# Attention and spectral feed-forward on one core: two weighted sums of a block issued back to back, and three GpSimd steps in other places

## The chip, the cores and the metric

One core of a Trainium2 chip runs the whole program. The time is the device time of one execution in microseconds (us). Engine names in the rows: PE is TensorE, PEld its weight loads, DVE is VectorE, ACT is ScalarE, POOL is GpSimd, SP is SyncE.

## The reference, cut to what matters

Two batches of 2048 tokens of width 512 attend to 128 context tokens with 16 heads, and a linear layer in the frequency domain follows; both have a layer norm ahead and a residual.

```python
q = layernorm(x) @ wq + bq;  k = ctx @ wk + bk;  v = ctx @ wv + bv       # 16 heads of 32
score = where(q k^T / sqrt(32) * mask == 0, -1e9, q k^T / sqrt(32) * mask)
x = x + (softmax(score) @ v) @ wo + bo
y = real(ifft(fft(layernorm(x)) @ (w_real + i w_imag)))                  # one real 512 x 512 matrix
x = x + y + bias
```

## The kernel before

The tokens are cut into 16 blocks (c = 0 to 15) of 256. A block has 4 **groups** of 4 heads, numbered s = 4c + g over the whole program, 64 in all. All large products are split into float16 high and low parts (names ending in h and l), three products for one.

The order of work is written out by hand. `plan()` makes a table of **slots** v, one for each group and some before and behind; four slots, r = v mod 4 = 0 to 3, make one block's period. Each engine's program loops over the same slots and has its own list of steps in each. A group s passes through them so:

- PE computes its scores (`scores`, L628) in slot s - 1 into the tile `scores`, of which there is one. DVE multiplies by the mask (`mask_mul`, L970), replaces zeros (`zero_to_neg`, L977, both inputs in SBUF) and takes minima (`least`, L982) in slot s. GpSimd turns the minima into `nbias` (`bias`, L1264). ACT takes exponentials (`exps`, L745, two calls of four instructions) in slot s + 1; one half of them lies before, the other behind the copies named next.
- PE transposes the result (`turn`, L642) in slot s + 2, and ACT copies it to `pt` (`copy_pt`, L754).
- Two groups make one **context** m = s // 2: PE forms the weighted sum of values (`weigh`, L656; eight fp32 products with 32 columns each, which the trace shows as 16 records) in slot 2m + 3, so one in each slot with r = 1 and r = 3. It goes to a PSUM bank of its own, `CX`. The reciprocals of the row sums are taken by DVE (L988), spread by GpSimd (`spread`, L1271, tile `rzb`), transposed by PE (the fill "R", L584) and copied by ACT (`copy_rec`, L761). In slot 2m + 5 DVE multiplies (`ctx_norm`, L995, tile `cn`), ACT casts to the high half (`ctx_hi`, L768, tile `ch`), GpSimd forms the low half (`ctx_lo`, L1277, tile `cl`).

Between these PE runs **fills**, each a group of products into one of three PSUM banks taken in turn, so that fill n may start only when the bank of fill n - 3 has been read by DVE (semaphore `g_free`, counted in the order of fills). In one period they are: r = 0: "WO" 0 and "R"; r = 1: "WO" 1 and "QQ"; r = 2: "FF" 0 and "R"; r = 3: "FF" 1, for most blocks "ST", and "QQ". "WO" is the output projection of block c - 2 (L478, 12 products), "FF" the feed-forward of block c - 3 (L478), "QQ" the query projection of a later block (L483, 24 products), "ST" a small product of statistics (L491). A fill "QQ" is read in the slot behind its own: ACT casts it to `qh` (L719), and then DVE forms `ql` (L942), which frees the bank.

GpSimd's other steps are the sums with the bias of the output projection (`add_bo`, L1216, on `xs`), with the last bias (`add_bf`, L1250, on `x1`), low halves (`split_lo` L1207, `norm_lo2` L1239), and small ones for the statistics (`rstd2`: L1223 and L1226). In slots 4 to 63 it waits for `zero_to_neg` of the slot before most of its steps.

Of the kernel before, what the change touches and what calls it, by code (L numbers as in the profile page):

```python
# [5 lines left out]
ALU = mybir.AluOpType  # L6
# [31 lines left out]
def plan():  # L38

    fills, slots, held = [], {}, []
    lead = [("CT", 0), ("CT", 1), ("K", 0), ("K", 1), ("W1", 0), ("ST", 0), ("Q", 0, 0), ("Q", 0, 1), ("S", 0),
            ("W1", 1), ("Q", 0, 2), ("Q", 0, 3), ("S", 1), ("ST", 1), ("Q", 1, 0), ("Q", 1, 1), ("S", 2),
            ("Q", 1, 2), ("Q", 1, 3)]
    front = []
    for f in lead:
        if f[0] == "S":  # L50
# [8 lines left out]
    }  # L59
    queries = {2: (2, 0), 4: (2, 1), 5: (3, 0), 6: (3, 1)}  # L60
    for v in range(V0, V1):
        c, r = divmod(v, 4)
        mid = {
            0: [("WO", c - 2, 0)],
            1: [("WO", c - 2, 1)],
            2: [("FF", c - 3, 0)],
            3: [("FF", c - 3, 1)],
        }[r]
        mid = [f for f in mid if 0 <= f[1] < NC] + early.get(v, [])
        mid = {NS - 4: [("FF", NC - 4, 0)], NS - 3: [("WO", NC - 3, 1)], NS - 2: [], NS - 1: [("FF", NC - 3, 0)],  # L70
               NS: [("WO", NC - 2, 0)], NS + 1: [("WO", NC - 2, 1)], NS + 2: [("FF", NC - 3, 1)], NS + 3: []}.get(v, mid)
# [12 lines left out]
        if v in queries:  # L84
            late.append(("QQ",) + queries[v])
        elif v >= 7 and v % 2 == 1 and (v + 9) // 4 < NC:
            late.append(("QQ", (v + 9) // 4, (v + 9) % 4 // 2))
        base = len(fills)
        fills += mid + late
        mids = list(range(base, base + len(mid)))  # L90
        lates = list(range(base + len(mid), len(fills)))
        items = []
        if 0 <= v - 2 < NS:
            items += [("PT", v - 2, 0), ("PT", v - 2, 1)]
        items += [("G", n) for n in mids]
        if 0 <= v + 1 < NS:
            items += [("S", v + 1, 0), ("S", v + 1, 1)]
        if v % 2 == 1 and 0 <= v - 3 < NS:
            items += [("PV", (v - 3) // 2)]
        items += [("G", n) for n in lates]  # L100
        slots[v] = (items, [n for n in held if fills[n][0] in ("R", "ST")],
                    [n for n in held if fills[n][0] not in ("R", "ST")], [n for n in mids if fills[n][0] != "R"])
        held = lates
    return fills, front, slots


def row_slot(c):
# [21 lines left out]
def build(nc, x, xt, ctx_in, mask, wq, bq, wk, bk, wv, bv, wo, bo, lparts, tables, bf, eye, sums, pick, places, heads, out):  # L129
# [3 lines left out]
    with ExitStack() as stack:  # L133
# [337 lines left out]
        def _(pe):  # L471
# [22 lines left out]
            def fill(n):  # L494
# [84 lines left out]
                elif kind == "R":  # L579
                    pe.wait_ge(p_rz, c + 1)  # L580
                    for i in range(2):
                        for t in range(2):
                            a = 256 * i + 128 * t
                            last = pe.transpose(o[:, a:a + 128], rzb[:, i, 4 * t:4 * t + 4, :], ident[:])  # L584
                elif kind == "WO":
                    pe.wait_ge(o_lo, 2)
                    pe.wait_ge(ch_done, min(2 * c + 2, NS // 2 - 1))
# [54 lines left out]
                        last = pe.transpose(PB[f][:, a:a + 128], zs[:, s % NZ, t, 2 * f + i, :], ident[:])  # L642
                last.then_inc(pt_done, 1)

            def weigh(m):
                c, h = divmod(m, 2)
                b = c // (NC // NB)
                pe.wait_ge(pt_copied, 4 * m + 4)
                if m >= 1:
                    pe.wait_ge(cn_done, m)  # L650
                else:
                    pe.wait_ge(g_free, at["V", 0] + 1)
                for i in range(2):
                    for j in range(4):
                        n = 32 * (8 * h + 4 * i + j)
                        last = pe.matmul(CX[32 * j:32 * j + 32, 256 * i:256 * i + 256], vs[:, b, n:n + 32],  # L656
                                         pt[:, i, j, :], start=True, stop=True)
                last.then_inc(pv_done, 1)

            def zeros(count):  # L660
                for i in range(count):
# [17 lines left out]
        def _(act):  # L679
# [69 lines left out]

            def copy_pt(s, f):  # L750
                act.wait_ge(pt_done, 2 * s + f + 1)
                if f == 0 and s >= 2:
                    act.wait_ge(pv_done, s // 2)
                act.copy(pt[:, s % 2, 2 * f:2 * f + 2, :], PB[f][:]).then_inc(pt_copied, 1)  # L754

            def copy_rec(m):
                n = at["R", m]
                act.wait_ge(g_done, n + 1)
                if m >= 1:
                    act.wait_ge(cn_done, m)  # L760
                act.copy(rec[:], bank_of(n)[:].rearrange("p (i n) -> p i n", i=2)).then_inc(rc_done, 1)  # L761

            def ctx_hi(m):
                c, h = divmod(m, 2)
                act.wait_ge(cn_done, m + 1)
# [58 lines left out]
            for v in range(V0, V1):  # L824
# [35 lines left out]
                    exps(v - 1, 1)  # L860
                if v == 8:
                    exps(v, 0)
                if v % 2 == 1 and 0 <= v - 5 < NS - 2:
                    ctx_hi((v - 5) // 2)
                if v == NS + 1:
                    norm_hi2(NC - 2, 0)
                    copy_rec(NS // 2 - 1)
                    norm_hi2(NC - 2, 1)
                    last_ctx_hi()
# [16 lines left out]
        def _(dve):  # L886
# [102 lines left out]

            def ctx_norm(m):  # L990
                dve.wait_ge(rc_done, m + 1)
                dve.wait_ge(pv_done, m + 1)
                if m >= 1:
                    dve.wait_ge(p_cl, m)
                dve.tensor_tensor(cn[:], CX[:].rearrange("p (i n) -> p i n", i=2), rec[:], ALU.mult).then_inc(cn_done, 1)  # L995

            def last_ctx_norm():
                m = NS // 2 - 1
                dve.wait_ge(rc_done, m + 1)
                dve.wait_ge(pv_done, m + 1)  # L1000
# [105 lines left out]
            for v in range(V0, V1):  # L1106
# [3 lines left out]
                    mask_mul(v)  # L1110
                if v == NS + 1:
                    recip(NS // 2 - 1)
                if v % 2 == 1 and 0 <= v - 5 < NS - 2:
                    ctx_norm((v - 5) // 2)
                for n in prompt:
                    lo(n)
                if 0 <= v < NS:
# [57 lines left out]
        def _(pool):  # L1175
# [166 lines left out]
            for v in range(V0, V1):  # L1342
# [37 lines left out]
                for a in range(5, NC):  # L1380
                    if v == 4 * a - 11 and v != 13:
                        split_lo(a, slice(0, 2), False)
                    if v == 4 * a - 10 and v != 14:
                        split_lo(a, slice(2, 4))
                for a in range(2, 14):
                    if bo_slot(a) == v:
                        add_bo(a, 0)
                if v == 52:
                    add_bo(12, 1)
# [184 lines left out]
```

## Time and profile before

| | |
|---|---|
| time, median of 3 runs (lowest to highest) | 437.15 us (437.01 to 437.19) |
| the profiled execution: time, span | 437.58 us, 435.8 us |
| busy: PE, DVE, ACT, POOL | 430.0, 398.6, 365.2, 355.4 us |
| granted TensorE clock | 1.00 of full speed |

Busy is the time in which at least one instruction of the engine ran. The span is the time from the first to the last instruction of the profiled execution. A start in a timeline is counted from the start of the span; an instruction's time on DVE, ACT and POOL overlaps the start of the next one by up to 0.1 us, so steps are best read from start to start.

### The profile page before, as it was taken

What the parts mean: (1) busy time and instruction counts of PE and PEld (TensorE: products, weight loads), DVE (VectorE), ACT (ScalarE), POOL (GpSimd) and SP (SyncE); (2) the same over time, 40 slices, a digit from 0 to 9 for tenths busy, and PEclk for the clock granted to TensorE, in tenths of its full rate; (3) what the DMA queues carried; (4) which work ended last, traced back from release to release, by engine and by line L of the source; (5) the groups of instructions that cost most, each with busy time, mean ns of one, the idle gap of its engine ahead of it and who ended that gap; (6) DMA issues with size and microseconds to landing.
All of it is one profiled execution on the core that took longest, in us unless ns stands there. A gap on an engine that the chain in (4) does not pass through costs nothing.

```text
span 435.8 us, 10928 instructions
## 1 busy us (share of the span) xinstructions
PE 430.0 (99%) x3496; PEld 298.5 (69%) x3496; DVE 398.6 (91%) x535; ACT 365.2 (84%) x1341; POOL 355.4 (82%) x484
## 2 busy tenths in 40 slices
PE   7999999999999999999999999999999999999997
PEld 6897688787766776667676677666667765656544
DVE  3799899999999999999999999999999899999663
ACT  1768998989898999999899998999898898999820
POOL 5579988877999898989989898989899865675793
DMA  8999854403443855455455454445442434231144
GB/s 272 396 386 250 299 168 121 117 0 98 101 136 91 200 96 145 123 126 138 125 146 138 126 144 121 100 118 148 109 110 68 102 85 106 72 98 49 50 114 128
DMA packets 85286, 60.15 MB, mean 138 GB/s; under 512 B 40141, under 2 KB 72813, under 8 KB 84718
## 3 DMA queue, kind: packets, MB, share of 16 engines
q1 hardware_dynamic: 84508, 59.29, 49.6%
q8 instruction: 29, 0.48, 0.5%
q14 instruction: 27, 0.22, 0.2%
q10 hardware_dynamic: 722, 0.17, 0.2%
HBM read 29.33 MB, written 8.39 MB: 87 GB/s over the span
## 4 chain that ended last, share of the span: by engine, by line
PE 94%; DVE 2%; ACT 1%; issue 1%; POOL 1%; DVEq 0%; POOLq 0%
PE bank L478 36%; PE bank L483 24%; PE bank L642 12%; PE bank L656 7%; PE scores L628 6%; PE bank L584 3%; PE bank L565 2%; PE scores L483 1%; PE bank L662 1%; ACT zs L745 1%; PE bank L491 1%; DVE zs L977 1%; DVE nmin L982 0%; PE bank L505 0%; ACT pt L754 0%
## 5 line engine op out<-in xcount | busy, mean ns | idle before, releaser
L745 ACT ACTIVATE zs<-zs,nbias 128x128 f32<-128x128 f32 x512 | 199.7, 397 | 13.3 <-POOL nbias L1264 12.9
L745 ACT ACTIVATION_READ_ACCUMULATOR zs<-zs,nbias 128x1 f32 x512 | 99.4, 194 | 0.0
L977 DVE SCALAR_TENSOR_TENSOR zs<-zs 128x1024 f32<-128x1024 f32 x64 | 88.9, 1389 | 1.1
L982 DVE TENSOR_REDUCE nmin<-zs 128x8 f32<-128x1024 f32 x64 | 78.0, 1219 | 2.1
L970 DVE TENSOR_TENSOR zs<-scores,ms 128x1024 f32<-128x1024 f32 x64 | 78.0, 1218 | 0.1
L754 ACT COPY pt<-bank 128x512 f32<-128x512 f32 x128 | 67.9, 582 | 8.2 <-PE bank L642 8.0
L642 PE MATMUL bank<-ident,zs 128*128 128x128 f32 x512 | 66.7, 273 | 0.1
L1216 POOL TENSOR_TENSOR xs<-xs,bob 128x512 f32<-128x512 f32 (+1 forms) x41 | 43.4, 1059 | 22.9 <-DVE zs L977 22.8
L483 PE MATMUL bank<-xth,wqh 128*128 128x256 f16 x224 | 61.2, 273 | 0.0
L483 PE MATMUL bank<-xth,wql 128*128 128x256 f16 x224 | 61.1, 273 | 0.0
L483 PE MATMUL bank<-xtl,wqh 128*128 128x256 f16 x224 | 61.1, 273 | 0.0
L642 PEld LDWEIGHTS bank<-ident,zs 128*128 128x128 f32 x512 | 57.6, 140 | 3.6 <-ACT zs L745 1.7
L478 PE MATMUL bank<-woh,ch 128*128 128x512 f16 x128 | 48.5, 379 | 0.6 <-POOL cl L1277 0.6
L478 PE MATMUL bank<-wol,ch 128*128 128x512 f16 x128 | 48.5, 379 | 0.0
L478 PE MATMUL bank<-woh,cl 128*128 128x512 f16 x128 | 48.5, 379 | 0.0
L478 PE MATMUL bank<-mh,x1h 128*128 128x512 f16 x120 | 45.5, 379 | 0.0
L478 PE MATMUL bank<-ml,x1h 128*128 128x512 f16 x120 | 45.5, 379 | 0.0
L478 PE MATMUL bank<-mh,x1l 128*128 128x512 f16 x120 | 45.5, 379 | 0.0
L1239 POOL TENSOR_TENSOR x1nl<-x,x1nh 128x512 f16<-128x512 f32 x30 | 35.8, 1194 | 9.6 <-DVE zs L977 9.6
L1250 POOL TENSOR_TENSOR x<-x,bfb 128x512 f32<-128x512 f32 x32 | 41.1, 1286 | 1.4 <-DVE zs L977 1.2
L628 PEld LDWEIGHTS scores<-ks,qs 102*128 102x128 f16 (+1 forms) x480 | 31.9, 98 | 13.2 <-issue 0.2
L1271 POOL COPY rzb<-rz 128x512 f32<-128x512 f32 x32 | 38.5, 1202 | 2.0 <-DVE rz L988 1.7
(130 smaller groups left out, 906.3 us busy)
## 6 DMA issues: line engine op xcount, KB each, us to landing
xs<-in_x SPq DMA_DIRECT2D x16, 512.0 KB, 4.4
xtr<-in_xt SPq DMA_DIRECT2D x16, 512.0 KB, 4.8
out<-x SPq DMA_DIRECT2D x31, 256.0 KB, 2.5
qs<-qh SPq DMA_DIRECT2D x120, 64.0 KB
lp<-in_lparts SPq DMA_DIRECT2D x4, 1024.0 KB, 9.8
qs<-ql SPq DMA_DIRECT2D x60, 64.0 KB
ms<-in_mask SPq DMA_DIRECT2D x16, 128.0 KB, 2.4
wks<-in_wk SPq DMA_DIRECT2D x2, 512.0 KB, 6.2
```

Of the source, the lines that this page charges most:

```text
L478: last = pe.matmul(o, a, b, start=(i == 0), stop=(i == len(mm) - 1))
L483: last = pe.matmul(o, a, b, start=(first and i == 0), stop=(i == len(pairs) - 1))
L628: last = pe.matmul(A[:, n % 2, 128 * j:128 * j + 128], qs[c % 2][0:rows, g, j, 128 * t:128 * t + 128], ks[0:rows, g, j, c // (NC // NB), : ...
L642: last = pe.transpose(PB[f][:, a:a + 128], zs[:, s % NZ, t, 2 * f + i, :], ident[:])
L745: last = act.activation(z, z, ACT.Exp, bias=nbias[:, s % 4, i:i + 1], scale=-NEG, accum_out=zsum[:, s % 4, i:i + 1])
L754: act.copy(pt[:, s % 2, 2 * f:2 * f + 2, :], PB[f][:]).then_inc(pt_copied, 1)
L970: dve.tensor_tensor(zs[:, s % NZ], A[:].rearrange("p t (h k) -> p t h k", h=4), ms[:, c % NM].unsqueeze(2).broadcast_to([128, 2, 4, KEYS]) ...
L977: dve.scalar_tensor_tensor(out=z, in0=z, scalar=0.0, in1=z, op0=ALU.is_equal, op1=ALU.subtract).then_inc(eq_done, 1)
L982: dve.tensor_reduce(nmin[:, s % 4, :], zs[:, s % NZ].rearrange("p t h k -> p (t h) k"), AX.X, ALU.min).then_inc(mn_done, 1)
L1216: i = pool.tensor_tensor(z, z, bob[:, n], ALU.add)
L1250: pool.tensor_tensor(z, z, bfb[:], ALU.add).then_inc(p_x1b, 1)
L1271: pool.tensor_copy(rzb[:].rearrange("p i h w -> p (i h) w"), rz[:, z, :].rearrange("p i h -> p (i h)").unsqueeze(2).broadcast_to([128, 16, ...
```

## The change

For blocks 3 to 12 the weighted sum of the first context (m = 2c) no longer stands in slot 4c + 3. It is now a fill "P" in slot 4c + 5, straight ahead of the weighted sum of the second context (m = 2c + 1), and writes to one of the three banks that the fills share; the second still goes to `CX`. A second buffer `ptb` holds the transposed exponentials of every other context. `ctx_norm`, `ctx_hi` and `ctx_lo` of the first context move one slot on, from 4c + 5 to 4c + 6. On GpSimd `ctx_lo` of the second context now stands ahead of `bias` in slot 4c + 7; `add_bo(c, 0)` of blocks 4 to 11 moves from slot 4c + 3 to slot 4c + 5, and `add_bf(c - 3, 1)` from r = 1 to r = 2.

```diff
+PAIRED = range(3, 13)
+LATE_BO = range(4, 12)
...
+        both = [("P", (v - 5) // 4)] if r == 1 and (v - 5) // 4 in PAIRED else []
...
-        fills += mid + late
+        fills += mid + both + late
...
+        items += [("G", base + len(mid))] * len(both)
-        if v % 2 == 1 and 0 <= v - 3 < NS:
+        if v % 2 == 1 and 0 <= v - 3 < NS and not in_fill((v - 3) // 2):
             items += [("PV", (v - 3) // 2)]
...
+def in_fill(m):
+    return m % 2 == 0 and m // 2 in PAIRED
...
+def in_pair_end(v):
+    return v % 4 == 3 and (v - 7) // 4 in PAIRED
...
+def late_bf(v):
+    return VT <= v < NS or v // 4 - 1 in LATE_BO
...
+        ptb, _ = sb("ptb", [128, 2, 4, CH], F32, a_wv)
+        pts = [pt, ptb]
...
+                elif kind == "P":
+                    last = weighted(2 * c, o)
...
-                if f == 0 and s >= 2:
-                    act.wait_ge(pv_done, s // 2)
+                if f == 0 and s >= 4:
+                    wait_weighed(act, s // 2 - 2)
...
-                if v % 2 == 1 and 0 <= v - 5 < NS - 2:
+                if v % 2 == 1 and 0 <= v - 5 < NS - 2 and not in_fill((v - 5) // 2):
                     ctx_hi((v - 5) // 2)
+                if v % 2 == 0 and in_fill((v - 6) // 2):
+                    ctx_hi((v - 6) // 2)
...
+                if v % 2 == 0 and in_fill((v - 6) // 2):
+                    ctx_norm((v - 6) // 2)
...
+                if in_pair_end(v):
+                    ctx_lo((v - 5) // 2)
                 for a in range(2, 14):
-                    if bo_slot(a) == v:
+                    if bo_slot(a) == v and a not in LATE_BO:
                         add_bo(a, 0)
...
+                if v % 2 == 0 and in_fill((v - 6) // 2):
+                    ctx_lo((v - 6) // 2)
...
+                if r == 1 and c - 1 in LATE_BO:
+                    add_bo(c - 1, 0)
-                if r == 2 and VT <= v < NS:
+                if r == 2 and late_bf(v):
                     add_bf(c - 3, 1)
```

The order of instructions on three engines shows where this puts them. The line numbers of the changed kernel are other ones: 668 for 628, 692 for 656, 521 for 483, 788 for 745, 797 for 754, 811 for 768, 762 for 719, 780 for 737, 804 for 761, 1325 for 1277, 1312 for 1264, 1287 for 1239, 1264 for 1216, 1319 for 1271.

On PE, in slot 33 (r = 1), from the last scores on; before:

```order
L478 MATMUL bank<-woh,cl 128x512
L628 MATMUL scores<-ks,qs_63 128x128 x8
L656 MATMUL bank<-pt,vs 32x256 x8
L483 MATMUL bank<-xth,wqh 128x256
L483 MATMUL bank<-xth,wql 128x256
```

and of the change:

```order
L516 MATMUL bank<-woh,cl 128x512
L668 MATMUL scores<-ks,qs_63 128x128 x8
L692 MATMUL bank<-pt,vs 32x256 x8
L692 MATMUL bank<-ptb,vs 32x256 x8
L521 MATMUL bank<-xth,wqh 128x256
```

Eight products more stand between the scores and "QQ"; in slot 35 (r = 3) the same eight are gone from between the scores and "ST".

On ACT, in slot 34 (r = 2), from the copies of `pt` on; before:

```order
L754 COPY pt<-bank 128x512 x2
L745 ACTIVATE zs,zsum<-zs,nbias 128x128 x4
L719 CAST qh<-bank 128x512
L737 CAST x1nh<-x_76 128x512
L761 COPY rec<-bank 128x512
```

and of the change:

```order
L797 COPY pt<-bank 128x512 x2
L788 ACTIVATE zs,zsum<-zs,nbias 128x128 x4
L811 CAST ch<-cn 128x512
L762 CAST qh<-bank 128x512
L780 CAST x1nh<-x_76 128x512
L804 COPY rec<-bank 128x512
```

The cast of `ch` (`ctx_hi` of the first context) now stands ahead of the cast of `qh`; it is gone from slot 33.

On POOL, the end of slot 34 and slot 35 (r = 3); before:

```order
L1239 TENSOR_TENSOR x1nl<-x_76,x1nh 128x512
L1216 TENSOR_TENSOR xs<-xs,bob 128x256
L1216 TENSOR_TENSOR xs<-xs,bob 128x512
L1264 TENSOR_SCALAR nbias<-nmin 128x8
L1277 TENSOR_TENSOR cl<-cn,ch 128x512
L1239 TENSOR_TENSOR x1nl<-x_76,x1nh 128x512
L1216 TENSOR_TENSOR xs<-xs,bob 128x256
L1271 COPY rzb<-rz 128x512
```

and of the change:

```order
L1325 TENSOR_TENSOR cl<-cn,ch 128x512
L1287 TENSOR_TENSOR x1nl<-x_76,x1nh 128x512
L1298 TENSOR_TENSOR x_76<-x_76,bfb 128x512
L1264 TENSOR_TENSOR xs<-xs,bob 128x256
L1325 TENSOR_TENSOR cl<-cn,ch 128x512
L1312 TENSOR_SCALAR nbias<-nmin 128x8
L1287 TENSOR_TENSOR x1nl<-x_76,x1nh 128x512
L1264 TENSOR_TENSOR xs<-xs,bob 128x256
L1319 COPY rzb<-rz 128x512
```

Slot 34 has a low half `cl` and an `add_bf` more. In slot 35 the sum of 512 columns on `xs` is gone, and the second context's `cl` stands ahead of `nbias`.

## Rows read from the trace of the kernel before

**Rows 1.** The page's engines, and its chain that ended last, by engine.

```profile
PE 430.0 (99%) x3496; PEld 298.5 (69%) x3496; DVE 398.6 (91%) x535; ACT 365.2 (84%) x1341; POOL 355.4 (82%) x484
...
PE 94%; DVE 2%; ACT 1%; issue 1%; POOL 1%; DVEq 0%; POOLq 0%
```

**Rows 2.** Windows of one period: length, busy per engine, clock, DMA.

```profile
243.07:267.17 24.10, 24.10 (x205) 16.50 (x203) 23.43 (x31) 22.00 (x83) 21.32 (x29) 1.00 0.48 129
```

**Rows 3.** Timeline, PE, slots 32 to 37: start, us, line, operation.

```profile
226.33 0.61 PE L628 MATMUL scores<-ks,qs 102*128 102x128 f16 x8
226.78 0.60 PE L584 MATMUL bank<-ident,rzb 128*128 128x128 f32 x4
...
230.68 0.61 PE L628 MATMUL scores<-ks,qs 102*128 102x128 f16 x8
231.22 1.07 PE L656 MATMUL bank<-pt,vs 128*32 128x256 f32 x16
232.23 0.28 PE L483 MATMUL bank<-xth,wqh 128*128 128x256 f16 x1
...
234.86 1.04 PE L642 MATMUL bank<-ident,zs 128*128 128x128 f32 x8
...
252.19 0.38 PE L478 MATMUL bank<-woh,ch 128*128 128x512 f16 x1
...
254.78 0.39 PE L628 MATMUL scores<-ks,qs 102*128 102x128 f16 x4
```

**Rows 4.** Timeline, PE, first half of the sum at 231.22.

```profile
231.22 0.64 PE L656 MATMUL bank<-pt,vs 128*32 128x256 f32 x8
```

**Rows 5.** Timeline, ACT, slots 34 to 36; idle before in brackets.

```profile
238.00 0.57 ACT L719 CAST qh<-bank 128x512 f16<-128x512 f32 x1
...
239.41 0.59 ACT L761 COPY rec<-bank 128x512 f32<-128x512 f32 x1 [0.32 <-PE bank L584]
...
244.06 0.61 ACT L768 CAST ch<-cn 128x512 f16<-128x512 f32 x1
...
245.28 0.40 ACT L745 ACTIVATE zs<-zs,nbias 128x128 f32<-128x128 f32 x1 [0.33 <-POOL nbias L1264]
...
247.60 1.07 ACT L754 COPY pt<-bank 128x512 f32<-128x512 f32 x2 [0.68 <-PE bank L642]
...
250.11 0.57 ACT L719 CAST qh<-bank 128x512 f16<-128x512 f32 x1
```

**Rows 6.** Timeline, POOL, slot 35.

```profile
245.01 0.23 POOL L1264 TENSOR_SCALAR nbias<-nmin 128x8 f32<-128x8 f32 x1
245.21 1.16 POOL L1277 TENSOR_TENSOR cl<-cn,ch 128x512 f16<-128x512 f32 x1
246.32 1.16 POOL L1239 TENSOR_TENSOR x1nl<-x,x1nh 128x512 f16<-128x512 f32 x1
247.45 0.72 POOL L1216 TENSOR_TENSOR xs<-xs,bob 128x256 f32<-128x256 f32 x1
```

**Rows 7.** Timeline, DVE, slots 34 to 37.

```profile
238.61 0.69 DVE L942 TENSOR_TENSOR ql<-bank,qh 128x512 f16<-128x512 f32 x1
...
240.70 1.22 DVE L970 TENSOR_TENSOR zs<-scores,ms 128x1024 f32<-128x1024 f32 x1
...
246.33 1.23 DVE L970 TENSOR_TENSOR zs<-scores,ms 128x1024 f32<-128x1024 f32 x1
247.59 1.66 DVE L977 SCALAR_TENSOR_TENSOR zs<-zs 128x1024 f32<-128x1024 f32 x1
...
250.72 0.69 DVE L942 TENSOR_TENSOR ql<-bank,qh 128x512 f16<-128x512 f32 x1 [0.21 <-ACT qh L719]
...
252.88 1.23 DVE L970 TENSOR_TENSOR zs<-scores,ms 128x1024 f32<-128x1024 f32 x1
```

**Rows 8.** One line's instructions (L977, L1271): count, ns min/median/max.

```profile
L977 DVE SCALAR_TENSOR_TENSOR zs<-zs x64: 1215/1228/2311, 25.8 to 401.6; 128x1024 f32<-128x1024 f32 x64
...
L1271 POOL COPY rzb<-rz x32: 602/1602/1617, 48.9 to 411.9; 128x512 f32<-128x512 f32 x32
```

More of the change, by code:

```diff
@@ L87, in plan @@
             late.append(("QQ", (v + 9) // 4, (v + 9) % 4 // 2))
+        both = [("P", (v - 5) // 4)] if r == 1 and (v - 5) // 4 in PAIRED else []
         base = len(fills)
-        fills += mid + late
+        fills += mid + both + late
         mids = list(range(base, base + len(mid)))
-        lates = list(range(base + len(mid), len(fills)))
+        lates = list(range(base + len(mid + both), len(fills)))
         items = []
@@ L104, in plan, with own @@
     return fills, front, slots
+def in_fill(m):
+    return m % 2 == 0 and m // 2 in PAIRED
+def own(m):
+    return m + 1 - sum(in_fill(i) for i in range(m + 1))
 def row_slot(c):
@@ L294, in cast_count, with wait_weighed, wait_context @@
             return n + 1 - min(n + 1, 2) - min(max(n + 1 - tile_of(12, 0), 0), 4)
+        def wait_weighed(eng, m):
+            if in_fill(m):
+                eng.wait_ge(g_done, at["P", m // 2] + 1)
+            else:
+                eng.wait_ge(pv_done, own(m))
+        def wait_context(eng, m):
+            if in_fill(m):
+                eng.wait_ge(g_free, at["P", m // 2] + 1)
+            else:
+                eng.wait_ge(cn_done, own(m))
         def columns(n):
@@ L643, in turn, with weighted @@
                 last.then_inc(pt_done, 1)
-            def weigh(m):
+            def weighted(m, o):
                 c, h = divmod(m, 2)
@@ L648, in weigh @@
                 pe.wait_ge(pt_copied, 4 * m + 4)
[L649 to L652, printed above, removed]
                 for i in range(2):
@@ L655, in weigh @@
                         n = 32 * (8 * h + 4 * i + j)
-                        last = pe.matmul(CX[32 * j:32 * j + 32, 256 * i:256 * i + 256], vs[:, b, n:n + 32],
-                                         pt[:, i, j, :], start=True, stop=True)
-                last.then_inc(pv_done, 1)
+                        last = pe.matmul(o[32 * j:32 * j + 32, 256 * i:256 * i + 256], vs[:, b, n:n + 32],
+                                         pts[m % 2][:, i, j, :], start=True, stop=True)
+                return last
+            def weigh(m):
+                if m >= 1:
+                    pe.wait_ge(cn_done, own(m) - 1)
+                else:
+                    pe.wait_ge(g_free, at["V", 0] + 1)
+                weighted(m, CX).then_inc(pv_done, 1)
             def zeros(count):
@@ L751, in copy_pt @@
                 act.wait_ge(pt_done, 2 * s + f + 1)
-                if f == 0 and s >= 2:
-                    act.wait_ge(pv_done, s // 2)
-                act.copy(pt[:, s % 2, 2 * f:2 * f + 2, :], PB[f][:]).then_inc(pt_copied, 1)
+                if f == 0 and s >= 4:
+                    wait_weighed(act, s // 2 - 2)
+                act.copy(pts[s // 2 % 2][:, s % 2, 2 * f:2 * f + 2, :], PB[f][:]).then_inc(pt_copied, 1)
             def copy_rec(m):
@@ L759, in copy_rec @@
                 if m >= 1:
-                    act.wait_ge(cn_done, m)
+                    wait_context(act, m - 1)
                 act.copy(rec[:], bank_of(n)[:].rearrange("p (i n) -> p i n", i=2)).then_inc(rc_done, 1)
@@ L764, in ctx_hi @@
                 c, h = divmod(m, 2)
-                act.wait_ge(cn_done, m + 1)
+                wait_context(act, m)
                 if h == 0 and c >= 2:
@@ L991, in ctx_norm @@
                 dve.wait_ge(rc_done, m + 1)
-                dve.wait_ge(pv_done, m + 1)
+                wait_weighed(dve, m)
                 if m >= 1:
                     dve.wait_ge(p_cl, m)
-                dve.tensor_tensor(cn[:], CX[:].rearrange("p (i n) -> p i n", i=2), rec[:], ALU.mult).then_inc(cn_done, 1)
+                src, done = (bank_of(at["P", m // 2]), g_free) if in_fill(m) else (CX, cn_done)
+                dve.tensor_tensor(cn[:], src[:].rearrange("p (i n) -> p i n", i=2), rec[:], ALU.mult).then_inc(done, 1)
             def last_ctx_norm():
@@ L999, in last_ctx_norm @@
                 dve.wait_ge(rc_done, m + 1)
-                dve.wait_ge(pv_done, m + 1)
+                dve.wait_ge(pv_done, own(m))
                 dve.wait_ge(p_cl, m)
@@ L1112, in _ @@
                     recip(NS // 2 - 1)
-                if v % 2 == 1 and 0 <= v - 5 < NS - 2:
+                if v % 2 == 1 and 0 <= v - 5 < NS - 2 and not in_fill((v - 5) // 2):
                     ctx_norm((v - 5) // 2)
+                if v % 2 == 0 and in_fill((v - 6) // 2):
+                    ctx_norm((v - 6) // 2)
                 for n in prompt:
@@ L1428, in _ @@
                     norm_lo2(c - 2, 0)
-                elif v % 2 == 1 and 2 <= v - 5 < NS - 2:
+                elif v % 2 == 1 and 2 <= v - 5 < NS - 2 and not in_fill((v - 5) // 2) and not in_pair_end(v):
                     ctx_lo((v - 5) // 2)
+                if v % 2 == 0 and in_fill((v - 6) // 2):
+                    ctx_lo((v - 6) // 2)
                 if v == NS + 1:
@@ L1441, in _ @@
                     norm_lo2(c - 2, 1)
-                if v not in (NS - 4, NS + 1) and r < 2 and 0 <= c - 3 < NC and v > 13 and not (r == 1 and VT <= v < NS):
+                if v not in (NS - 4, NS + 1) and r < 2 and 0 <= c - 3 < NC and v > 13 and not (r == 1 and late_bf(v)):
                     add_bf(c - 3, r)
-                if r == 2 and VT <= v < NS:
+                if r == 1 and c - 1 in LATE_BO:
+                    add_bo(c - 1, 0)
+                if r == 2 and late_bf(v):
                     add_bf(c - 3, 1)
```

## The prediction

> **What bounds the kernel now.** I read the page's engines and its chain first: PE is busy for 430.0 of 435.8 us and holds 94% of the chain [rows 1]. Then the windows of one period, four slots: 24.10 us, PE busy in all of it at full clock, but DVE busy for 23.43 and ACT for 22.00 [rows 2]. So a microsecond taken from PE is worth one only as far as DVE and ACT can come forward with it. The reader should look for that in the timelines: how much idle time they have, and how early they hand over what PE needs next. The place is "WO" 1 of r = 1 (slot 37). It needs the bank in which "QQ" of slot 35 lay, which DVE frees with `ql`. That ends at 250.72 + 0.69 = 251.41, and PE starts at 252.19: 0.78 us to spare [rows 3, 7]. The scores behind it (254.78) need the mask product that starts at 252.88 and ends at 254.11: 0.67 us [rows 3, 7]. I take this period for all ten.
>
> **What the change takes from PE.** In slot 35, "QQ" or "ST" follows the scores at once. Without a weighted sum, the next operation starts 0.45 us after the scores do (226.33 to 226.78), with one 1.55 (230.68 to 232.23) [rows 3]: 1.10 us gone. In slot 33, eight products more stand in a sum that is already under way. The first 8 of its 16 records end after 0.64 us and all 16 after 1.07 [rows 4, 3], so 8 records cost 0.43, 16 more 0.86; entering and leaving the narrow products is paid once. A period then has 1.10 - 0.86 = 0.24 us less on PE, and ten pairs 2.4 us. That is all the change can give.
>
> **What it does to the two others.** I count from the transpositions of r = 2, PE at 234.86, as zero, because ACT waits for them there before and after: with the pair ahead of "QQ" they come 0.86 later than other work of the slot.
>
> ACT: `qh` starts at 3.14 [rows 5]. The change puts `ch` (0.61, of which 0.10 overlaps the next) ahead of it: 3.65. DVE's `ql` follows `qh` by 0.61 (238.00 to 238.61), so it moves from 3.75 to 4.26 [rows 5, 7]. On ACT the delay is taken up soon: the copy of `rec` at 239.41 had 0.32 idle before it [rows 5], and about 0.1 of delay remains, which the wait for `nbias` behind it covers. The cast `ch` of the second context then stands where it stood, at 9.20. Behind it comes the moved step of GpSimd. Before, `nbias` started at 245.01 (10.15) and did not depend on `ch`; now the low half `cl` goes first and waits for `ch`. It ends at 9.81; I add 0.08 for the signal (an estimate: the ACT to DVE signal of the `ql` row is 0.04), 1.11 for `cl` (245.21 to 246.32), and have `nbias` at 11.00; exponentials follow 0.27 later (245.01 to 245.28) at 11.27, against 10.42 now [rows 5, 6]. That is 0.85 late. Four exponentials take 1.55 (from 245.28 to the idle time ahead of 247.60, less overlap), so the copy of `pt` starts at 12.8; now it starts at 12.74 after waiting 0.68 for PE [rows 5]. That wait is gone, as PE comes 1.10 earlier there, and `nbias` has eaten it. `qh` 2.51 later (247.60 to 250.11) and `ql` another 0.61 later stands at **15.95, against 15.86 now**.
>
> DVE has the same answer by its own row: `ql` at 4.26, 7.72 to the mask product of slot 36 (238.61 to 246.33), 1.26 to L977, then L977, L982 and `ql` [rows 7]. L977 is stretched there now, 1.66 where its least is 1.22 [rows 7, 8]. At its start (247.59) a GpSimd sum still ran until 248.17 [rows 6], 0.58 us, and the stretch is 0.44. After the change GpSimd's `rzb` copy of 0.60 [rows 8] should start about 0.25 ahead of L977 (`nbias` 11.00, then 0.2, 1.13 and 0.7 for the three steps behind it, 13.0; L977 at 13.24), so 0.37 is left of it and, with the same 0.14 off, the stretch is 0.23. Then `ql` cannot start before 15.86 either.
>
> The Trainium skill's page "SBUF — State Buffer", section "Who interferes with whom", says that a DVE instruction with two SBUF inputs and a GpSimd instruction that reads SBUF exclude each other for the whole instruction. By that rule the stretch would be all of the 0.37, DVE would be ready at 16.0, and the total would be 0.5 us higher. The row of L977 agrees that the two exclude each other, but shows 0.44 of stretch for 0.58 of overlap, so the sum keeps the 0.23.
>
> So neither row moves, while PE has lost 1.10 us ahead of "WO" 1. The scores of slot 38 would start at 254.78 - 234.86 - 1.10 = 18.82. Their mask product starts 2.16 after `ql` (250.72 to 252.88) [rows 7] and takes 1.23: 15.95 + 2.16 + 1.23 = 19.34, with 0.04 for a signal 19.38. PE waits some **0.55 us in each period**, most of it already ahead of "WO" 1 (16.68 against 16.23). Queued behind are the scores, the pair, "QQ" and the next transpositions, for which ACT waits: the loop closes, and each period starts from the same state. A period takes 24.10 - 0.24 + 0.55 = 24.41 us.
>
> **The sum.** Ten places: nine full periods between the first and the last pair at 0.55, and the first (slot 17), where `ch` and `cl` are not moved yet, at 0.35 (between nothing and 0.55). -2.4 + 9 x 0.55 + 0.35 = +2.9 us. The profiled execution took 437.58 us with a span of 435.8; the median of the runs is 437.15, to which I add: **440.0 us**. The signals (0.03 to 0.1) and the roundings of a long row make the wait 0.40 to 0.67, which gives 438.7 to 441.1 for this case.
>
> What I cost at nothing: the bank of "P", which "WO" 0 held a slot earlier and "R" needs again only a slot later; DVE's moved `cn`, as DVE then waits for `qh` anyway; the moved `add_bo` and `add_bf`, hidden by GpSimd's idle time (355.4 of 435.8 us busy [rows 1]), with `xs` and `x` read slots later (if GpSimd is late, see rival 4); the second buffer `ptb`, which only takes a wait away. No DMA is moved, and SP's queue has the same order.
>
> **Rivals.** (1) *Faster.* ACT and DVE come forward after all: 0.55 us less between the transpositions and `ql`, and PE waits nowhere: 434.8 us. For it: ACT has 1.33 us idle in this stretch (0.32, 0.33, 0.68) [rows 5]. Against it: each of the three is spent above on `ch` and `cl`, and DVE has only 0.21 idle [rows 7]. It decides where the wait is under 0.24 per period, what PE saves. (2) *No change:* the wait is 0.15 to 0.33, about half of what I work out: -2.4 and ten times that give 436.3 to 438.0. (3) *The pair does not share its way in and out*, since it writes two banks and reads two buffers: the first sum costs 1.10 instead of 0.86, and 24.41 becomes 24.65: 442.4 us. For it: no two such sums stand together in the trace. Against: the bank and the buffer do not matter to the products of L478, which change both without a gap. (4) *GpSimd runs into L977 in r = 3.* Slot 34 has a `cl` (1.16 [rows 6]) and an `add_bf` more on GpSimd, and by the same kind of steps its last sum on `xs` ends some 0.1 ahead of L977 of slot 35 (an estimate). If it is 0.2 late it is still free; each tenth beyond that costs a tenth, up to 0.6 (the 0.72 of that sum less 0.14), each period: up to 445 us.
>
> **Chances.** The forecast 0.53; (3) or (4), slower still, 0.12; (2) 0.14, of which some ends on either side; (1) 0.21. What a measurement can tell from no change is about 0.2%, 0.9 us. Slower by more 0.65, within it 0.14, faster by more 0.21. The range leaves out a tenth on each side: the lower end stands inside rival (1), with part of the waits left (435.4), the upper end at rival (3), 442.6.
>
> **What the profile after would show.** PE idle of about 0.4 ahead of L516's first product in r = 1 and 0.1 to 0.2 ahead of the scores, every 24.4 us; the removed sum leaving 0.45 between scores and "ST"; the pair taking 1.93 us from its first start to its last end; ACT without idle time from the copy of `pt` in r = 2 to `ch`, then about 1.2 us of waiting for `nbias`; `qh` 15.3 after the transpositions. I am wrong if PE stays without idle time and the period is 23.86, or if `nbias` in r = 3 is not behind `cl`.

## The result, and the profile after

| | before | after |
|---|---|---|
| time, median of 6 runs each (lowest to highest) | 437.08 us (436.55 to 437.22) | 444.21 us (443.08 to 445.48) |
| ratio, 95% interval | | 1.0167 [1.0142, 1.0191] |
| the profiled execution: time, span | 437.58, 435.8 us | 445.31, 443.5 us |
| granted TensorE clock of the profiled execution | 1.00 | 0.996 |

The change makes the kernel 7 us slower. I had forecast slower, but 440.0 us and 442.6 at most. The six runs of after fall in two groups: three have a granted clock of 0.996 (445.05, 445.31, 445.48 us) and three one of 1.0 (443.08, 443.18, 443.36 us). One of the sixteen runs of the kernel before that were taken beside e8 and e9 (below) took 905.53 us, and the ratios leave it out.

Read first the page's engines and its chain by engine, against [rows 1]:

```profile
PE 433.2 (98%) x3496; PEld 298.9 (67%) x3496; DVE 393.4 (89%) x535; ACT 362.4 (82%) x1341; POOL 348.2 (79%) x484
...
PE 49%; DVE 25%; ACT 10%; issue 10%; POOL 4%; DMA 1%; DVEq 0%; SPq 0%; ACTq 0%; POOLq 0%
```

PE held 94% of the chain and now holds 49%. DVE, ACT and POOL are no busier than before; they are later. The table of waits says for what (engine and line, what it waited for: us in total, times, longest):

```profile
ACT zs L788 <- POOL nbias L1312: 26.6, 24, 3.5
POOL cl L1325 <- ACT ch L811: 23.4, 21, 3.1
DVE ql L987 <- ACT qh L762: 17.0, 12, 3.5
```

Two of the three are the steps of the forecast: the exponentials behind `nbias`, and `cl` behind `ch`. The longest wait of the exponentials, 3.5 us, is far above the 1.2 that I worked out for one period. So I read a steady period and the last place apart. Windows of after: the period that answers to [rows 2], from the scores of slot 37 to those of slot 41, then the one from slot 53 to slot 57:

```profile
251.34:275.80 24.46, 24.35 (x203) 16.44 (x202) 22.94 (x31) 21.67 (x83) 20.24 (x30) 1.00 0.50 128
349.19:376.32 27.13, 24.38 (x193) 15.55 (x192) 20.96 (x27) 22.02 (x86) 15.40 (x23) 0.94 0.37 79
```

Eight such periods in a row, from the scores of slot 21 to those of slot 53, are 24.45 to 24.47 us long (forecast: 24.41). The last is 27.13, and its granted clock is 0.94.

The steady period on PE, from the scores of slot 37 on (timeline; compare [rows 3]):

```profile
251.34 0.61 PE L668 MATMUL scores<-ks,qs 102*128 102x128 f16 x8
251.79 0.61 PE L622 MATMUL bank<-ident,rzb 128*128 128x128 f32 x4
252.40 1.09 PE L682 MATMUL bank<-ident,zs 128*128 128x128 f32 x8
253.60 0.39 PE L516 MATMUL bank<-woh,ch 128*128 128x512 f16 x1
...
256.29 0.62 PE L668 MATMUL scores<-ks,qs 102*128 102x128 f16 x8
256.84 1.07 PE L692 MATMUL bank<-pt,vs 128*32 128x256 f32 x16
257.73 1.05 PE L692 MATMUL bank<-ptb,vs 128*32 128x256 f32 x16
```

The second sum starts 0.89 behind the first (0.86 forecast): the way in and out is shared. From "R" to the transpositions it is 0.61 us, on to "WO" 1 1.20, on to the scores 2.69. In a kernel without the wait (e6, below) these are 0.44, 0.88 and 2.59. PE therefore waits 0.17 + 0.32 + 0.10 = 0.59 us, little of which counts as idle time of PE: in the waits of this stretch it stands with the weight loads (0.2 for ACT's exponentials, 0.3 for `ql`, 0.4 for the mask product). The forecast had nothing ahead of the transpositions and about 0.45 ahead of "WO" 1.

ACT and POOL of the same stretch (compare [rows 5, 6]):

```profile
240.02 0.61 ACT L811 CAST ch<-cn 128x512 f16<-128x512 f32 x1
240.53 0.58 ACT L762 CAST qh<-bank 128x512 f16<-128x512 f32 x1
...
246.05 0.62 ACT L811 CAST ch<-cn 128x512 f16<-128x512 f32 x1
...
248.20 0.40 ACT L788 ACTIVATE zs<-zs,nbias 128x128 f32<-128x128 f32 x1 [1.26 <-POOL nbias L1312]
...
249.76 1.04 ACT L797 COPY ptb<-bank 128x512 f32<-128x512 f32 x2
...
252.25 0.57 ACT L762 CAST qh<-bank 128x512 f16<-128x512 f32 x1
```

```profile
246.81 1.16 POOL L1325 TENSOR_TENSOR cl<-cn,ch 128x512 f16<-128x512 f32 x1 [1.89 <-ACT ch L811]
247.94 0.23 POOL L1312 TENSOR_SCALAR nbias<-nmin 128x8 f32<-128x8 f32 x1
```

The transpositions of slot 34 start at 236.88 here. Counted from there `qh` comes at 15.37 (forecast 15.34). DVE (compare [rows 7]) has `ql` at 252.85, which is 15.97 (15.95), and L1022 takes 1.49 (1.45):

```profile
250.12 1.49 DVE L1022 SCALAR_TENSOR_TENSOR zs<-zs 128x1024 f32<-128x1024 f32 x1
...
252.85 0.69 DVE L987 TENSOR_TENSOR ql<-bank,qh 128x512 f16<-128x512 f32 x1
```

Now the last place, slots 51 to 54; POOL, ACT, and PE:

```profile
344.66 1.16 POOL L1325 TENSOR_TENSOR cl<-cn,ch 128x512 f16<-128x512 f32 x1 [0.85 <-ACT ch L811]
345.78 1.27 POOL L1264 TENSOR_TENSOR xs<-xs,bob 128x512 f32<-128x512 f32 x1
347.02 1.21 POOL L1312 TENSOR_SCALAR nbias<-nmin 128x8 f32<-128x8 f32 x1
```

```profile
348.25 0.40 ACT L788 ACTIVATE zs<-zs,nbias 128x128 f32<-128x128 f32 x1 [3.47 <-POOL nbias L1312]
```

```profile
350.05 0.63 PE L622 MATMUL bank<-ident,rzb 128*128 128x128 f32 x4 [0.24 <-POOL rzb L1319]
352.45 1.97 PE L682 MATMUL bank<-ident,zs 128*128 128x128 f32 x8 [1.78 <-ACT zs L788]
354.21 0.64 PE L516 MATMUL bank<-woh,ch 128*128 128x512 f16 x1
354.64 0.64 PE L516 MATMUL bank<-wol,ch 128*128 128x512 f16 x1
...
357.52 0.61 PE L668 MATMUL scores<-ks,qs 102*128 102x128 f16 x8
```

Between `cl` and `nbias` stands a sum of 512 columns that is in no other such slot: `add_bo(12, 0)`. The change moves these sums for blocks 4 to 11 only, but pairs the sums of blocks 3 to 12. It puts `nbias` off by 1.24 us, into DVE's L1022 (346.40 to 348.13), where the step of 0.23 takes 1.21. ACT waits 3.47 us, and PE 1.78 ahead of the transpositions. Behind this idle time PE runs at half speed for some 3 us in this execution: its products start every 0.43 us where 0.22 is usual, and the transpositions take 1.97 instead of 1.04. The window of this stretch has the granted clock, 0.50:

```profile
352.45:355.60 3.15, 3.15 (x12) 2.26 (x13) 2.63 (x5) 3.15 (x12) 1.15 (x5) 0.50 0.57 120
```

### The profile page after: what moved, and what is told of

Same layout as the page of the kernel before. It is cut to its first block, busy times and chain, and to the rows that moved or that the text cites. A ratio compares the mean times of both kernels' runs of the same rounds, so it can differ in the third digit from the quotient of the medians.

```text
span 443.5 us, 10926 instructions
## 1 busy us (share of the span) xinstructions
PE 433.2 (98%) x3496; PEld 298.9 (67%) x3496; DVE 393.4 (89%) x535; ACT 362.4 (82%) x1341; POOL 348.2 (79%) x484
## 4 chain that ended last, share of the span: by engine, by line
PE 49%; DVE 25%; ACT 10%; issue 10%; POOL 4%; DMA 1%; DVEq 0%; SPq 0%; ACTq 0%; POOLq 0%
PE bank L516 17%; PE bank L521 14%; DVE zs L1022 7%; PE bank L692 6%; ACT zs L788 6%; PE bank L682 5%; DVE zs L1015 4%; DVE nmin L1027 3%; DVE x L1000 3%; DVE st L1073 3%; PE bank L603 2%; PE scores L668 2%; DVE ql L987 2%; ACT pt L797 2%; DVE cn L1041 2%
## 5 line engine op out<-in xcount | busy, mean ns | idle before, releaser
L788 ACT ACTIVATION_READ_ACCUMULATOR zs<-zs,nbias 128x1 f32 x512 | 100.8, 197 | 0.0
L1022 DVE SCALAR_TENSOR_TENSOR zs<-zs 128x1024 f32<-128x1024 f32 x64 | 83.9, 1311 | 1.1
L1027 DVE TENSOR_REDUCE nmin<-zs 128x8 f32<-128x1024 f32 x64 | 78.0, 1219 | 2.1
L682 PE MATMUL bank<-ident,zs 128*128 128x128 f32 x512 | 68.1, 277 | 2.5 <-ACT zs L788 2.4
L1325 POOL TENSOR_TENSOR cl<-cn,ch 128x512 f16<-128x512 f32 x31 | 36.0, 1161 | 25.0 <-ACT ch L811 23.4
L1264 POOL TENSOR_TENSOR xs<-xs,bob 128x512 f32<-128x512 f32 (+1 forms) x41 | 44.5, 1086 | 6.0 <-DVE zs L1022 5.9
L1255 POOL TENSOR_TENSOR xtl<-xtr,xth 128x512 f16<-128x512 f32 (+1 forms) x27 | 35.1, 1303 | 11.7 <-DVE zs L1022 8.4
L797 ACT COPY pt<-bank 128x512 f32<-128x512 f32 x64 | 34.1, 586 | 9.1 <-PE bank L682 9.0
```

The costliest lines, as they stand in the source:

```text
L788: last = act.activation(z, z, ACT.Exp, bias=nbias[:, s % 4, i:i + 1], scale=-NEG, accum_out=zsum[:, s % 4, i:i + 1])
L797: act.copy(pts[s // 2 % 2][:, s % 2, 2 * f:2 * f + 2, :], PB[f][:]).then_inc(pt_copied, 1)
L1022: dve.scalar_tensor_tensor(out=z, in0=z, scalar=0.0, in1=z, op0=ALU.is_equal, op1=ALU.subtract).then_inc(eq_done, 1)
L1027: dve.tensor_reduce(nmin[:, s % 4, :], zs[:, s % NZ].rearrange("p t h k -> p (t h) k"), AX.X, ALU.min).then_inc(mn_done, 1)
L1264: i = pool.tensor_tensor(z, z, bob[:, n], ALU.add)
L1325: pool.tensor_tensor(cl[:, c % 2, 2 * h:2 * h + 2, :], cn[:], ch[:, c % 2, 2 * h:2 * h + 2, :], ALU.subtract).then_inc(p_cl, 1)
```

## The experiments

All are cut from the changed kernel. **A** is my reading; **the offset** is the start of the scores of slot 63 against the kernel before, with both traces laid on each other at slot 12.

| kernel | time, us (runs) | ratio to before [95%] | steady period, us | offset, us |
|---|---|---|---|---|
| after | 444.21 (6) | 1.0167 [1.0142, 1.0191] | 24.46 | +7.80 |
| e1 | 441.72 (4) | 1.0114 [1.0100, 1.0128] | 24.46 | +4.45 |
| e2 = e1 + `nbias` first | 442.32 (4) | 1.0145 [1.0124, 1.0166] | 24.62 | +5.23 |
| e3 = e1 + `qh` first | 441.15 (4) | 1.0103 [1.0089, 1.0117] | 24.46 | +4.43 |
| e4 = e2 + e3 | 439.09 (5) | 1.0060 [1.0047, 1.0072] | 24.22 | +2.14 |
| e5 = after, sums early | 453.39 (1) | 1.037 (one run) | 25.70 | +16.54 |
| e6 = e4 + order of GpSimd | 436.80 (11) | 0.9989 [0.9978, 1.0000] | 23.86 | -0.30 |
| e7 = e6, pairs 3 to 11 | 436.14 (6) | 0.9973 [0.9961, 0.9984] | 23.86 | -0.96 |
| e8 = e6, no pairs | 437.68 (11) | 1.0015 [0.9998, 1.0031] | 24.10 | +0.73 |
| e9 = e6, pairs 4 to 11 | 435.62 (6) | 0.9970 [0.9957, 0.9983] | 23.86 | -1.50 |

**e1: the sum of block 12 behind `nbias`.**

```diff
-                    if bo_slot(a) == v and a not in LATE_BO:
+                    if bo_slot(a) == v and a not in LATE_BO and a != 12:
...
                     bias(v)
+                if v == 51:
+                    add_bo(12, 0)
```

> The changed kernel with one step moved: the bias sum of block 12 (512 columns on xs) stands behind nbias of slot 51 on GpSimd, not between the low half cl and nbias. Theory A (the period of slots 18 to 50 is right as forecast, 24.41 forecast and 24.46 measured, and the rest of the miss is this one place, where ACT waits 3.47 us for nbias): the wait falls by about 2.2 us to some 1.3 as in the other periods, the late transpositions of slot 53 come about 2 us earlier, no fall of the clock: 440.6 to 441.3 us. Theory B (the excess of slot 53 comes from something else, the end of the pairs): 443 or more.

POOL of e1 in slot 51, and PE in slot 53:

```profile
345.50 0.23 POOL L1312 TENSOR_SCALAR nbias<-nmin 128x8 f32<-128x8 f32 x1
345.70 1.27 POOL L1264 TENSOR_TENSOR xs<-xs,bob 128x512 f32<-128x512 f32 x1
```

```profile
350.23 1.04 PE L682 MATMUL bank<-ident,zs 128*128 128x128 f32 x8
```

The wait of 1.78 us and the lower clock are both gone, and 3.35 us of the offset with them. The time, 441.72, is 0.4 above the 440.6 to 441.3 expected. The two traces are 0.29 apart at the scores of slot 53 (349.19 and 348.90). So `nbias` ends 348.23 - 345.73 - 0.29 = 2.21 us earlier and the transpositions start 352.45 - 350.23 - 0.29 = 1.93 us earlier; the other 1.4 come behind them. How much of it is the clock's is read from e5 (below), which has the same wait without the fall. The rest, +4.45, is made elsewhere, and the period is unchanged.

**e2, e3, e4: the two rows.** e2 puts `cl` of the second context behind `nbias` again in slots with r = 3; e3 puts `ch` of the first behind `qh` in slots with r = 2; e4 does both.

In e2:

```diff
-                if in_pair_end(v):
-                    ctx_lo((v - 5) // 2)
...
                     bias(v)
+                if in_pair_end(v):
+                    ctx_lo((v - 5) // 2)
```

and in e3:

```diff
-                if v % 2 == 0 and in_fill((v - 6) // 2):
-                    ctx_hi((v - 6) // 2)
...
                     for n in held:
                         hi(n)
+                if v % 2 == 0 and in_fill((v - 6) // 2):
+                    ctx_hi((v - 6) // 2)
```

> As e1, and nbias ahead of the second context's low half again in r = 3. Theory A (ACT's row and DVE's row arrive together: DVE has no idle time ahead of ql of r = 0 even now): the wait of ACT for nbias in r = 3 falls from 1.26 to about 0.4, but the period only from 24.46 to about 24.39, time 0.5 to 1 us under e1. Theory B (that wait is what holds PE): the period falls to the 23.9 that PE needs, time about 436.

> As e1, and ACT casts qh of r = 2 ahead of the first context's ch. Theory A: DVE's row comes 0.35 to 0.5 us forward, ACT's row does not; period 24.40 to 24.46, time within 0.7 us of e1. Theory B (the delay of qh by ch is what holds PE): period about 24.0, time about 437.

> Both edits of e2 and e3 on e1. Theory A (two rows side by side, each enough alone to hold PE): only here does the period fall, by 0.3 to 0.5 us to about 24.0, time 436.5 to 438. If either edit alone did all, this one adds nothing to it.

e3 alone leaves the period as it was (24.46), as its theory A had it. e2 alone makes the period *longer*, by 0.16, which neither of its theories expected; ACT's wait for `nbias` fell to 0.94 us, not to 0.4. POOL and then DVE of e2:

```profile
247.20 0.23 POOL L1312 TENSOR_SCALAR nbias<-nmin 128x8 f32<-128x8 f32 x1 [2.70 <-issue]
247.40 1.17 POOL L1325 TENSOR_TENSOR cl<-cn,ch 128x512 f16<-128x512 f32 x1
...
249.63 0.74 POOL L1264 TENSOR_TENSOR xs<-xs,bob 128x256 f32<-128x256 f32 x1
250.30 1.62 POOL L1319 COPY rzb<-rz 128x512 f32<-128x512 f32 x1
```

```profile
249.71 1.74 DVE L1022 SCALAR_TENSOR_TENSOR zs<-zs 128x1024 f32<-128x1024 f32 x1
```

The scores of slot 37 start at 251.30 here and at 251.34 in after, so the rows compare directly. `nbias` is 0.74 earlier (247.94 to 247.20), as it should be. But it still waits for DVE's minima, and while it does, POOL stands still where `cl` ran before. `cl` and all behind it come 0.4 to 0.6 later, so that the sum on `xs` now lies in L1022 (1.74 instead of 1.49) and `rzb` behind it takes 1.62: on PE "R" waits 0.15 for `rzb`, and "WO" 0 of slot 36 waits for `cl`:

```profile
248.71 0.38 PE L516 MATMUL bank<-woh,ch 128*128 128x512 f16 x1 [0.20 <-POOL cl L1325]
```

It starts 1.24 behind the transpositions (247.47), where 0.87 is usual: 0.37 lost, against 0.20 won from the scores of slot 37 to those of slot 38 (4.75 us, 4.95 in after). The wait for `cl` is thus what makes the period longer.

With both rows mended (e4) the period is 24.22, not the 24.0 expected, and the time 439.09, above the 436.5 to 438: 0.24 of the 0.60 is back, but 0.36 is left. DVE and POOL of e4 say why:

```profile
248.06 1.73 DVE L1022 SCALAR_TENSOR_TENSOR zs<-zs 128x1024 f32<-128x1024 f32 x1
```

```profile
243.01 1.73 POOL L1264 TENSOR_TENSOR xs<-xs,bob 128x256 f32<-128x256 f32 x1
...
247.99 0.72 POOL L1264 TENSOR_TENSOR xs<-xs,bob 128x256 f32<-128x256 f32 x1
248.66 1.60 POOL L1319 COPY rzb<-rz 128x512 f32<-128x512 f32 x1
```

GpSimd meets L1022 in two neighbouring slots. A half sum that starts at 243.01 takes 1.73 us (0.74 is usual), but it ends 0.8 us before `nbias` starts (245.55) and holds up nothing here. The other, at 247.99, lies in the L1022 of slot 36, which takes 1.73 instead of 1.22, and `rzb` behind it takes 1.60. On PE the 0.36 stands from the scores of slot 37 on: "R" starts 0.72 behind them (249.69 to 250.41) where 0.45 is usual, as it waits for `rzb`, and the next scores another 0.08 late (254.40), when the mask product of 253.12 has ended. Neither theory of mine had this third cost.

**e5: all sums early.** `LATE_BO = range(0)` in the changed kernel: each `add_bo(c, 0)` stands between `cl` and `nbias`, as in slot 51, and `add_bf` is back in r = 1.

> The changed kernel with the two bias sums of blocks 4 to 11 back where the kernel before has them: the sum of 512 columns on xs in r = 3 ahead of nbias, and so behind the low half cl; add_bf in r = 1. Theory A (what stands between cl and nbias in r = 3 is paid by PE in full, as in slot 51): every period is 2 to 3.5 us longer than 24.46, the whole run 460 to 475 us. Theory B (slot 51 is a matter of the end of the pairs only): periods of about 24.5, 444 us.

The window of one period:

```profile
255.64:281.34 25.70, 24.54 (x203) 16.48 (x202) 22.95 (x31) 21.68 (x83) 20.25 (x30) 1.00 0.46 121
```

Every period is 1.24 us longer than in after, which is what the sum takes (345.78 to 347.02). A is right in kind, but the 460 to 475 us that I gave for it was too high (453.4): I had priced each place like slot 51, where the sum also pushed `nbias` into L1022 and the clock fell. In a steady period of e5 `nbias` is not caught, and PE waits 0.94 us in one piece, ahead of "R", with its clock at 1.00:

```profile
257.19 0.63 PE L622 MATMUL bank<-ident,rzb 128*128 128x128 f32 x4 [0.94 <-POOL rzb L1319]
```

The last place of e5 is that of after again: `nbias` takes 1.22 us, and the transpositions of slot 53 wait 1.79. But the clock does not fall; the transpositions, and a window behind their start as long as that of after:

```profile
361.72 1.09 PE L682 MATMUL bank<-ident,zs 128*128 128x128 f32 x8 [1.79 <-ACT zs L788]
361.72:364.87 3.15, 3.04 (x17) 1.75 (x18) 2.63 (x5) 3.15 (x12) 1.15 (x5) 1.00 0.57 120
```

So the length of this wait does not by itself decide whether the clock falls. It also gives the price of each part. From the scores of slot 53 to those of slot 54 it is 4.96 us in e1, 7.16 in e5 and 8.33 in after: 2.20 for the late `nbias` (its 2.21 above), 1.17 for the clock.

**e6: GpSimd's half sum ahead of `nbias`, and the spread behind L1022.** On top of e4. The half sum moves in the slots 15, 19, ... 47; `moved` holds for the slots 19, 23, ... 51, whose `spread` moves to the slot behind:

```diff
-                    if 4 * a + 3 == v and a > 2:
-                        add_bo(a, 1, slice(0, D // 2), False)
...
+                for a in range(3, 12):
+                    if 4 * a + 3 == v:
+                        add_bo(a, 1, slice(0, D // 2), False)
                 if 0 <= v < NS:
                     bias(v)
...
+                if moved(v - 1):
+                    pool.wait_ge(eq_done, v + 1)
+                    spread((v - 4) // 2)
```

> On e4, two GpSimd steps in other places in slots 19 to 51: the first half of the bias sum on xs (256 columns) of r = 3 ahead of nbias, where GpSimd waits, and the spread of the reciprocals (rzb) behind L977 of the next slot, so that no GpSimd step is under way when L977 of r = 0 starts. Theory A (in e4 DVE's row alone holds PE, by L977 taking 1.73 instead of 1.22): L977 of r = 0 takes 1.22 to 1.25, the period falls from 24.22 to 23.86 to 23.95, which is what PE needs, and the time to 435.5 to 436.5. Theory B (another wait stands right behind): the period stays above 24.1, time over 438.

Window of one period, then POOL and DVE:

```profile
249.11:272.97 23.86, 23.86 (x203) 16.60 (x202) 22.87 (x31) 21.77 (x83) 21.15 (x30) 1.00 0.49 130
```

```profile
242.43 2.40 POOL L1269 TENSOR_TENSOR xs<-xs,bob 128x256 f32<-128x256 f32 x2
244.90 0.23 POOL L1317 TENSOR_SCALAR nbias<-nmin 128x8 f32<-128x8 f32 x1
245.10 1.16 POOL L1330 TENSOR_TENSOR cl<-cn,ch 128x512 f16<-128x512 f32 x1
...
248.76 0.61 POOL L1324 COPY rzb<-rz 128x512 f32<-128x512 f32 x1 [1.38 <-DVE zs L1027]
```

```profile
247.47 1.23 DVE L1027 SCALAR_TENSOR_TENSOR zs<-zs 128x1024 f32<-128x1024 f32 x1
```

The period is 23.86, the 24.10 - 0.24 of my "I am wrong if", and PE is busy in all of it. The half sums fill the time in which GpSimd waits for the minima, and what stood behind them no longer meets L1022 (L1027 here), which takes its 1.23. The time, 436.80, is 0.3 above the 435.5 to 436.5 expected. As e6 moves two steps at once, it does not show which of them is needed.

**e7, e8, e9: which pairs.** `PAIRED = range(3, 12)`, `range(0)` and `range(4, 12)` in e6.

> As e6, but block 12 is not paired (nine pairs). Theory A (slots 51 to 54 have no room for the pair: e4 shows 0.8 us of wait ahead of the scores of slot 53's end): 0.3 to 0.9 us faster than e6, as the lost 0.24 is less than the wait. Theory B: 0.2 us slower than e6.

> The kernel of e6 with its steps of GpSimd and ACT where they stand there, but PAIRED = range(0): no pair, each weighted sum in its own slot as in the kernel before. Theory A (a pair gives 0.24 us on TensorE and nothing else, once the two other rows are mended): the r = 1 periods are 24.10 as in the kernel before, TensorE stays without idle time in them, and the time is that of the kernel before within 0.5 us (436.8 to 437.9). Rival B (what e6 and e7 gained came from the new order on GpSimd and not from the pairs): the period is 23.9 here too and the time 436.2 or less. Rival C (the new order costs something by itself, which a pair's gift covers): period above 24.15 and the time above 438.2.

> The kernel of e6 with PAIRED = range(4, 12), eight pairs; e7 has nine (3 to 11), e6 ten. In e6 and e7 the scores of slot 19 come 1.09 us later than in the kernel before, against a gain of 0.24 for each later pair. Theory A (the first pair, block 3, pays an entry: its steps fall on those of the start, and it costs more than 0.24): without it the time is lower than that of e7, 0.3 to 1.0 us less (435.2 to 435.8). Rival B (the entry is paid by whichever pair is first): the loss moves to slot 23, and with one pair fewer the time is 0.2 us above that of e7 (436.3).

Without pairs, the same order gives 24.10 in the steady periods (slots 21 to 45), as before; with them 23.86. So a pair is worth 0.24 us to the hundredth, and the new order by itself nothing in such a period (theory A of e8). Outside them it costs: the offset of e8 is +0.25 at slot 17, +0.36 at slot 50 and +0.73 from slot 53 on, and its time is 0.8 us above that of the kernel before beside it (437.68, 436.84), where theory A had allowed 0.5; the interval still holds 1. The eight pairs of e9 are worth 2.06 us against e8 (435.62), for 8 x 0.24 = 1.92. The pair of block 12 costs 0.66 (e6 against e7, by offset) and that of block 3 0.54 (e7 against e9) where 0.24 was to be won. At block 3's place GpSimd has a sum of 512 columns and a half one ahead of `nbias` and `cl` in e7 (1.95 us from 123.57), which no slot later has, and PE waits for that `cl`:

```profile
126.99 0.38 PE L521 MATMUL bank<-woh,ch 128*128 128x512 f16 x1 [1.16 <-POOL cl L1330]
```

e9 has the lowest time and offset, 0.3% below the kernel before. Its ratio can't be told from e7's; that e9 is the better rests on the offset of one trace each. Its chain that ended last is PE's again, 94% as in [rows 1].

## Why the forecast was right for a steady period and wrong in its number

**What held.** The change takes 0.24 us a pair from PE (e6 against e8). ACT and DVE do not come forward: `qh` at 15.37 for 15.34, `ql` at 15.97 for 15.95, the next scores at 256.29 - 236.88 = 19.41 for 19.38. PE's wait is 0.59 for 0.55 in a steady period, which is 24.46 for 24.41. That the place of `ch` and that of `cl` hold it together is shown by e1 to e4: `ch` behind `qh` alone gives nothing (24.46 both), `nbias` first alone costs 0.16, and both give 0.24. That `nbias` first alone should give 0.07, as I expected of e2, was wrong, for the wait for `cl`. One reading of the forecast is wrong without harm to the sum: DVE's row. L977 starts at 247.59 and DVE is ready for `ql` 2.92 later (250.72 less its 0.21 idle); 0.21 less of stretch makes it 2.71, and 13.24 + 2.71 is 15.95, not 15.86. It measured 2.73 (250.12 to 252.85), and DVE had no idle time ahead of `ql`.

**The step that failed** is "I take this period for all ten", and with it the last line of the sum, "nine full periods [...] at 0.55, and the first [...] at 0.35". I had read the new order on GpSimd in slot 35 and did not look whether slots 15 and 51 have it too. They don't: the early sums leave blocks 4 to 11, while the pairs go from 3 to 12, so at either end a sum of 512 columns stands ahead of `nbias`. By offsets of the scores, the forecast of +2.9 becomes +7.8 so:

- the first place (scores of slot 19, +0.73; -0.24 would be no wait): 0.97 of waiting for 0.35, so +0.62. Start to start, 0.65 of it is PE's "WO" 0 waiting for `cl` behind that sum (1.52 behind the transpositions of 125.18, where 0.87 is usual; 0.49 shows as idle), and 0.30 is "R" waiting for `rzb` (129.29 to 130.04):

```profile
126.70 0.38 PE L516 MATMUL bank<-woh,ch 128*128 128x512 f16 x1 [0.49 <-POOL cl L1325]
```

- nine steady places: slot 19 to slot 51, eight of them, is +2.81, or 0.59 of waiting each for 0.55; the ninth, by e1, is +0.37 for +0.31; so +0.4;
- the last place: +3.35 by e1, of which 2.2 are the late `nbias` (1.24 behind the sum, 0.98 in L1022) and 1.2 the clock, by e5;
- what is left, 0.5, lies behind the last pair (in e1 from +3.93 at slot 55 to +4.88 at slot 58 and back to +4.45 at slot 63). It hangs on the order in slot 55, where `cl` still stands ahead of `nbias`: with `nbias` first it is 0.25 (e2, +4.98 to +5.23), and with both rows mended 0.10 (e4, +2.04 to +2.14).

So the clock, for which the forecast had no term, is not what took it out of its range: in the runs whose clock stayed at 1.0 the time is 443.2, still above it. They are 2.1 us below the others, more than the 1.2 of the rows; the difference stays open. That the lower clock in the other two runs of its group fell at the same place is not shown, as only one of them has a trace.

**The rivals.** (3) did not happen: the second sum costs 0.89. (4) named the right kind of meeting, GpSimd against L977, with up to 445 us, but in each period and for another slot; in a steady period the stretch is 0.27 for my 0.23. What made the last place was the same kind of meeting once. (1), faster, was ruled out for this order; its 434.8 us is what e9's order comes near to (435.62).

**The rule on DVE and GpSimd.** I had weighed the Trainium skill's "SBUF — State Buffer", section "Who interferes with whom" (a DVE instruction with two SBUF inputs contends with a GpSimd instruction that reads SBUF, and the lock is exclusive), against the row and kept overlap less 0.14. Each new row agrees with the row and not with the whole overlap. After: `rzb` (249.92 + 0.61) lies in L1022 for 0.41, stretch 0.27. e2: 0.66, stretch 0.52. e4: 0.65, stretch 0.51. Whether the last 0.14 of a GpSimd record still holds anything, the rows don't show. With DVE's row at 15.95 the whole overlap would have meant 16.09 and some 1.4 us more in all, not the 0.5 of the forecast; the steady period measured 24.46 for the 24.41 of the forecast, so 0.05 and not 0.14 more.

## What to carry to other kernels

A steady period that is worked out right is half of a sum: look at the first and the last place one by one, and compare the sets of blocks for which each part of a change holds. When an engine stands in a chain between two others, putting its urgent step first helps only if that step is ready; here the low half ahead of it filled a wait, and only with other work moved into that wait, and the spread out of DVE's way (e6), did the period fall below the old one. Judge a change that frees the bounding engine together with the orders of its neighbours: the pairs gained nothing until three places in these orders were mended (e2, e3, e6), and then just their 0.24 us.

## What the runs showed of the hardware

- Behind a wait of 1.78 us in after, PE's granted clock stood at 0.50, the lower of its two levels (1.2 GHz), in a window of 3.15 us, and products started every 0.43 us instead of 0.22; against e5 this cost 1.2 us. Behind a wait of 1.79 us at the same place of e5, and behind each of its waits of 0.94 us, it stood at 1.00.
- A GpSimd step of 8 columns (`nbias`, 0.23 us) that started while DVE's instruction with two inputs in SBUF was under way took 1.21 and ended 0.10 us behind it (348.23, 348.13), and a copy of 0.61 took 1.60 to 1.62. The small step lost four times its own length.
- The other way round, DVE's instruction was stretched by the overlap with the GpSimd step that was already running, less 0.14 us, in the kernel before, after, e2 and e4 (overlaps of 0.41 to 0.66 us).
